# Linear bias attention: the values' projection moved into the first score slots

## The reference

```
qkv = x @ W_attn + b_attn
q, k, v = jnp.split(qkv, 3, axis=-1)             # each to B, T, H, D
att = jnp.einsum('bqhd,bkhd->bhqk', q, k) * scale
att = att / temperature
bias = slopes[:, None, None] * rel[None, :, :]   # rel = key position - query position
bias = jnp.where(causal[None, :, :], bias, -jnp.inf)
att = att + bias[None, :, :, :]
w = jax.nn.softmax(att, axis=-1)
y = jnp.einsum('bhqk,bkhd->bqhd', w, v).reshape(Bc, Tc, Cc)
return y @ W_proj + b_proj
```

## Time and profile before

| | |
|---|---|
| median of 3 runs | 1758.93 us (1758.31 to 1760.62) |
| the profiled execution | 1761.15 us, its span 1759.8 us |
| busy, share of the span | PE 92%, DVE 59%, ACT 51%, POOL 25% |
| mean granted clock of TensorE | 0.982 |
| the stage `l3_attn` in the span | about 1309 to 1454 us |

### The profile page before, as it was taken

The page is one execution under the profiler, slowest core; times in us unless marked ns, Lnnn a source line. Parts: engine busy times, 40 slices in busy tenths (PEclk is TensorE's granted clock), DMA queues, the critical chain, the costliest instruction groups (busy, mean ns, idle before and its releaser), DMA issues. The chain is left out here.

```text
span 1759.8 us, 22408 instructions
## 1 busy us (share of the span) xinstructions
PE 1624.3 (92%) x7539; PEld 830.7 (47%) x7541; DVE 1037.3 (59%) x2130; ACT 902.8 (51%) x1748; POOL 431.3 (25%) x545
## 2 busy tenths in 40 slices
PE   7999998999998789999898999999988989999997
PEld 3344444445664244444345555555533445455546
DVE  5732026483314568888956888888547725565515
ACT  2431214253333457777844778888532654555513
POOL 1000100000000145555411555565301102233300
PEclk9999998999999999999999999999998999999998
DMA  6000100001000000000126231111038202000000
GB/s 231 0 1 0 42 1 1 36 0 48 1 1 19 0 10 18 10 10 10 52 96 216 77 99 28 41 42 28 20 70 242 60 1 91 20 22 12 1 0 25
DMA packets 36664, 74.11 MB, mean 42 GB/s; under 512 B 4427, under 2 KB 23179, under 8 KB 35115
## 3 DMA queue, kind: packets, MB, share of 16 engines
q1 hardware_dynamic: 36550, 72.68, 13.0%
HBM read 55.79 MB, written 16.78 MB: 41 GB/s over the span
## 5 line engine op out<-in xcount | busy, mean ns | idle before, releaser
L2456 POOL TENSOR_TENSOR work<-work,arena_b 128x512 f32<-128x512 f32 x128 | 166.5, 1302 | 129.1 <-ACT work L2313 129.1
L2408 DVE CUSTOM_DVE_ANT_0 ctx_keys<-ps,arena_a 128x1024 f32<-128x1024 f32 x128 | 154.7, 1210 | 0.2 <-PE ps L2189 0.2
L2189 PE MATMUL ps<-identity,ctx_keys 128*128 128x128 f32 x1024 | 142.4, 280 | 10.8 <-ACT work L2313 6.8
L2295 ACT ACTIVATE ctx_keys<-ctx_keys,small 128x1024 f32<-128x1024 f32 x128 | 146.8, 1147 | 0.4 <-DVE small L2408 0.4
L2189 PEld LDWEIGHTS ps<-identity,ctx_keys 128*128 128x128 f32 x1024 | 116.8, 143 | 60.6 <-ACT ctx_keys L2295 20.9
L2420 DVE TENSOR_TENSOR work<-ps,arena_b 128x512 f32<-128x512 f32 x128 | 88.1, 688 | 36.8 <-PE ps L2189 35.4
L3308 POOL TENSOR_SCALAR ctx_keys<-ctx_keys,small 128x128 f32<-128x128 f32 (+3 forms) x128 | 67.0, 536 | 172.5 <-DVE small L3231 172.5
L2313 ACT ACTIVATE work<-ps 128x512 f32<-128x512 f32 x128 | 76.2, 595 | 57.6 <-PE ps L2189 56.0
L1984 POOL TENSOR_SCALAR work<-work 128x1024 f32<-128x1024 int32 x64 | 66.6, 1041 | 112.7 <-DVE work L1937 112.2
L1770 PE MATMUL ps<-work 64*128 64x512 f32 x256 | 72.8, 645 | 16.8 <-DVE work L1937 14.6
L214 ACT ACTIVATE norm_parts<-normed 128x1024 f32<-128x1024 f32 x24 | 25.4, 1056 | 119.7 <-DVE normed L207 119.7
(11 more groups left out here) (405 smaller groups left out, 3400.0 us busy)
## 6 DMA issues: line engine op xcount, KB each, us to landing
work<-parts_k_L_xattn SPq DMA_DIRECT2D x15, 384.0 KB, 4.0
arena_a<-in_mask SPq DMA_DIRECT2D x2, 2048.0 KB, 7.8
arena_b<-in_groupT SPq DMA_DIRECT2D x2, 2048.0 KB, 9.6
head_weights<-in_w_L_xattn SPq DMA_DIRECT2D x8, 449.0 KB, 3.3
arena_a<-in_w_l_attn SPq DMA_DIRECT2D x1, 3072.0 KB, 14.7
head_weights<-in_w_L_attn SPq DMA_DIRECT2D x8, 384.0 KB, 3.1
work<-parts_q_L_attn SPq DMA_DIRECT2D x8, 384.0 KB, 4.6
work<-parts_k_L_attn SPq DMA_DIRECT2D x8, 384.0 KB, 5.4
```

The lines of the kernel that those rows point to most:

```text
L2189: mm = pe.transpose(t_psum[z][:, kt * P:(kt + 1) * P], prob[i % NP][:, o:o + P], k.iden[:, :])
L2295: act.activation(p, p, ACT.Exp, scale=-1.0, bias=minmax[:, i % 8:i % 8 + 1], accum_out=sums[:, i % 8:i % 8 + 1]).then_inc(*exped.up())
L2408: dve.tensor_tensor_reduce(prob[i % NP], s_psum[i % NS], NEG[:, b, qt, :], -1.0, BIG * 3e8, OP.add, OP.min, minmax[:, i % 8:i % 8 + 1]).th ...
L2456: pool.tensor_tensor(p, p, GT[:, b, 4:8, qt * P:(qt + 1) * P], OP.mult).then_inc(*weighed_pool.up())
```

## The change

The values leave the list of jobs; the list itself goes, and the chunks run in order with the six banks in turn. `values_of(pe, t)` stands behind the scores of slots 0 to 7, where the beat was, and makes one tile of 128 tokens: two products as before, and a third of a row of 128 ones with the row of the bias, added in the same accumulation. The tiles go to banks 2 to 5, two in each. In slots 1, 3, 5 and 7 ScalarE copies a bank into `vh` (L2848 has a copy of the same shape); VectorE's adds of the bias are gone. Unit 0's first transposed scores wait for the four copies. VectorE writes the ones at the stage's start. In VectorE's list `ln.scale` for the second half now follows `finish(0)` directly, and `finish(5)` follows the subtraction of chunk 6. SyncE's and GpSimd's orders are untouched.

```diff
-    JOBS = CHUNKS[0:2] + [("v", 0, 0), ("v", 0, 1)] + CHUNKS[2:6] + [("v", 0, 2), ("v", 0, 3)] + CHUNKS[6:8]
+    ones = k.extra[0:1, 1856:1984]
...
 def tensor(pe):
...
-        for y, (what, m, j) in enumerate(JOBS):
-            ps = k.bank(RING[y % 6])
-            if y in (0, 4):
-                pe.wait_ge(*ln.out(1 + y // 4))
-            if y >= 6:
-                pe.wait_ge(*freed(y - 6))
...
-            if y == 1:
+        for x, (what, m, t0) in enumerate(CHUNKS):
+            if x in (0, 2):
+                pe.wait_ge(*ln.out(1 + x // 2))
+            if x >= 6:
+                pe.wait_ge(*plain(x - 6))
+            for c in range(DC):
+                mm = pe.matmul(k.bank(RING[x % 6]), W[what][:, c, m * P:(m + 1) * P], k.Hn[:, c, t0:t0 + S], start=c == 0,
+                               stop=c == 1)
+            mm.then_inc(*part.up())
+            if x == 1:
                 ln.var(pe, 1)
-        pe.wait_ge(*values(nk))
...
-                if s < LAG - 2:
-                    k.beat(o_bank, 1)
+                if s < B * nk:
+                    values_of(pe, s)
...
 def transposed(pe, u, late):
+        if u == 0 and not late:
+            pe.wait_ge(*values(nk))
...
+    def values_of(pe, t):
+
+        if t == 0:
+            pe.wait_ge(*tempered(3))
+        ps = k.bank(2 + t // 2)[:, t % 2 * D:(t % 2 + 1) * D]
+        for c in range(DC):
+            pe.matmul(ps, k.Hn[:, c, t * P:(t + 1) * P], W["v"][:, c, :], start=c == 0, stop=False)
+        pe.matmul(ps, ones, bv[0:1], start=False, stop=True).then_inc(*valued.up())
...
 def scalar(act):
+            if s < B * nk and s % 2:
+                act.wait_ge(*valued(s + 1))
+                if s == 1:
+                    act.wait_ge(*cleared(2))
+                act.activation(vh[:, s - 1:s + 1, :, 0:dh], k.bank(2 + s // 2).rearrange("p (k h d) -> p k h d", k=2, h=H),
+                               ACT.Copy).then_inc(*values.up())
...
 def vector(dve):
+        dve.memset(ones, 1.0).then_inc(*tempered.up())
...
+        for x, (what, m, _) in enumerate(CHUNKS):
+            if what == "q":
+                dve.wait_ge(*part(x + 1))
+                if x >= 3:
+                    dve.wait_ge(*low(x - 2))
+                dve.tensor_scalar(rest[x][0], k.bank(RING[x % 6]), bqk[:, m:m + 1], rt, OP.add, OP.mult).then_inc(*q_plain.up())
+            dve.wait_ge(*hi(x + 1))
+            dve.tensor_tensor(rest[x][1], rest[x][0], parts[x][:, 0, :], OP.subtract).then_inc(*rest1.up())
+            if x not in (0, 2, NC // 2):
+                finish(dve, x - 1)
+            if x == 1:
                 ln.scale(dve, 1)
+            if x in (1, NC // 2 - 1, NC - 1):
+                finish(dve, x)
```

More of the change, by code:

```diff
@@ L2664, in l3_attn @@
     part, valued, scored, turned, scored_t, pv, spread, final = k.signals("pe", 8)
-    k_plain, hi, top_out, top_hi, exped, gathered, logged, inverse = k.signals("act", 8)
-    q_plain, rest1, low, tempered, values, maxed, top_rest, top_low, resid, scaled = k.signals("dve", 10)
+    k_plain, hi, top_out, top_hi, exped, gathered, logged, inverse, values = k.signals("act", 9)
+    q_plain, rest1, low, tempered, maxed, top_rest, top_low, resid, scaled = k.signals("dve", 9)
     middle, cleared, top_mid, put = k.signals("pool", 4)
@@ L2670, in l3_attn @@
     unit = lambda u: (u // 8, u % 8 // 4, u % 4)
-    def freed(y):
-        what, _, j = JOBS[y]
-        return values(j + 1) if what == "v" else plain(CHUNKS.index(JOBS[y]))
     def sync(sp):
@@ L2846, in scalar @@
                     act.wait_ge(*low(x - 2))
-                y = JOBS.index(CHUNKS[x])
-                act.activation(rest[x][0], k.bank(RING[y % 6]), ACT.Identity, bias=bqk[:, 2 + m:3 + m]).then_inc(*k_plain.up())
+                act.activation(rest[x][0], k.bank(RING[x % 6]), ACT.Identity, bias=bqk[:, 2 + m:3 + m]).then_inc(*k_plain.up())
             act.wait_ge(*plain(x))
@@ L2904, in vector @@
         dve.wait_ge(*loaded(7))
[L2905 to L2931, removed]
+        for x, (what, m, _) in enumerate(CHUNKS):
[9 more added lines that the diff above has]
+            if x == 1:
                 ln.scale(dve, 1)
-        finish(dve, pending)
+            if x in (1, NC // 2 - 1, NC - 1):
+                finish(dve, x)
         for s in range(SLOTS):
```

## The result

Over 20 runs each the changed kernel took 1763.59 us (median, 1758.19 to 1766.90) and the kernel before 1759.89 us (1756.65 to 1762.99): ratio 1.0019, 95% interval 1.0012 to 1.0027, so 3.3 us slower (2.1 to 4.8), at the edge of the 0.2% that I had set for "no change". The forecast was 2.0 us slower, in a range of 1757.6 to 1763.6. Put on the median that the forecast started from, the measured ratio gives 1758.93 x 1.0019 = 1762.3 us for the 1760.9 forecast.

What follows compares the result with a forecast made beforehand. Bound: a chain through slots 0 to 4, last_piece, put_top and stores 6 and 7 to unit 0's exponential. Terms -3.3, +2.4, +2.2, +1.15, -0.5 sum to +2.0 us: 1760.9 us from 1758.93, range 1757.6 to 1763.6.

Steps and rivals of the forecast that it cites:

- The chain: Slots 0 to 4, transpose, last_piece, put_top, stores 6 and 7 set unit 0's first exponential (1355.98 us), hence the end.
- Part 1: Projections without the values: ln.scale 1.5 us earlier, VectorE's chain 1.8 us shorter, slot 0 3.3 us earlier.
- Part 2: TensorE's two gaps, before chunk 2 and behind chunk 7: clock falls priced at 1.2 us each, +2.4 us.
- Part 3: Slots lengthen to 2.2 us with the values, +2.2 us over four; slot 4's later transpose, +1.15 us.
- Part 4: Transfers: stores of chunk 1 up to fetch 2 move by +0.3 us, still ahead of the first maxima row.
- Part 5: The clock later, from 1345 us into the steady part: no fall from 1345 to 1360, -0.5 us taken.
- The transfers hold everything: Rival: neither gap costs, last_piece stays nearly as now, fetches and stores wait for each other; 1758.5 us, chance 0.25.
- The values hide wholly: Rival: the products cost the slots nothing, slot 4's first reduction 1.5 us earlier; 1755.7 to 1757.4 us, chance 0.10.
- The clock decides: Rival, TensorE from 1317 to slot 2: both gaps cost 1.7 us, lower clock reaches slots; +5.0, 1763.9 us, chance 0.15.

Runs made afterwards that it cites:

- e2: The changed kernel with 12 beats in the gap between chunks 1 and 2 and 13 more behind chunk 7; ratio 1.0018 to the kernel before.
- e9: The changed kernel with the bias product over 128 rows of 1/128 instead of one row of ones; ratio 1.001 to the kernel before.
- e1: The changed kernel without the product of the ones with the bias row (values lack their bias); ratio 1.001 to the kernel before.
- e3: The changed kernel with the first maxima row (put_top) issued behind the stores of chunk 7, ahead of fetch 3; ratio 1.0015 to the kernel before.
- e5: The changed kernel with fetch 4 issued behind the second maxima row instead of ahead of it; ratio 1.0007 to the kernel before.
- e12: The changed kernel with beats in both gaps, the bias product over 128 rows and fetch 4 behind the second maxima row; ratio 1.0001 to the kernel before.

## Why the prediction was nearly right, step by step

**The chain held up to the exponential of unit 0, not beyond.** last_piece moved by +3.18 us and SyncE's put_top with it (40.78 for 37.60); the exponential waited for the stores as before, and moved by 2.35. It moved less since the last store landed 0.8 us faster after its issue (49.27 - 45.80 for 46.92 - 42.63). But unit 4 moved by 3.02, more than the exponential, so "whatever moves 1355.98 moves the end, and nearly nothing else does" was wrong; part 4 has the other path.

**Part 1** held: -1.5 us forecast for ln.scale, -1.55 measured; -3.3 for slot 0 with the clock up, -2.98 in e2 and e9, so the shorter chain of VectorE gave 1.4 for the 1.8 forecast.

**Part 2**: the clock fell at the first gap in four of the five executions that left it open and untouched (the change, e1, e3, e5, not e9) and cost 1.70 us (26.87 - 25.17), at the second in one of five (e1), and cost 2.0 us (28.90 - 26.87). By these few, 1.4 + 0.4 = 1.8 us for the 2.4 that I took. Six of six earlier gaps had made me price both alike at 1.2: for the second, of 3.06 us, that was three times too much. The Trainium skill (TensorE: Matmul & The Clock Gate, section "Why this matters for your kernels") would have it fall as well; here it fell in one execution of five.

**Part 3 is the step that failed, by its size.** "With 1.36 us the next score starts at 1340.80 ... 2.2 us a slot": measured were 1.59 and 2.43. The upper bound of the bias product, 0.45, was no bound: it took 0.63, and by e1 a slot is 0.72 longer with it. The slots from 0 to 4 gave back 9.73 - 6.64 = 3.09 us for the 2.2 forecast, and behind slot 4 the transpose cost 1.37 for 1.15 (difference 3.12 us after the slot's first reduction for 1.74).

**Part 4 left a path out.** I followed the first maxima row and not the second. SyncE issues fetches 3 and 4 behind stores 6 and 7 and the second row behind them, in both kernels. In the kernel before, the row landed at 53.86, just ahead of its use:

```profile
1354.84 1.17 SPq L2708 DMA_DIRECT2D work<-extra  x2
DMA to landing us min/median/max: 6.7/6.9/6.9
```

In the changed kernel put_top, late by 3.18, moved stores 6 and 7 and fetches 3 and 4 with it: fetch 4's last transfer lands at 56.29 for 53.12, the row right behind it at 57.15 for 53.86, and TensorE waited 1.82 us at unit 4. e5, which takes fetch 4 from ahead of the row, removes this wait alone. That slot 9 issued the row later (49.93 for 45.77) is not what counted: in e9 it is issued 1.5 us sooner than in e2 and lands no sooner. So slots 5 to 8 were late for nothing, as I had written; the second row was late because the first one was, through the transfers that stand between them.

**Part 5** held in sign: no fall in slots 6 to 9, and none in units 1 to 3. The three units from unit 1 to 4 took 6.95 us with the wait of 1.8 in it, for 6.28 before: 1.15 us won for the 0.5 taken. But in the changed kernel the wait for the second row swallows it: the exponential of unit 4 stands 0.74 or 0.75 us behind the row's landing in the change, e2 and e9, and in e1 as well, where the clock did fall in units 1 to 3.

**The sum again**, with measured terms up to unit 4 in the changed kernel's execution: -2.98 (projections) + 1.70 (first gap) + 3.09 (slots) + 1.37 (transpose) - 0.83 (landing) + 1.82 (unit 4) - 1.15 (clock) = 3.02 us, as read directly, and 3.3 (2.1 to 4.8) in the runs. By the second row it is shorter: the row lands 3.29 us later, and 0.27 of this was slack in the kernel before. That the forecast of 2.0 came so near is in part luck: the projections, the slots, the transpose and the missing path made it too small by 0.3, 0.9, 0.2 and 1.8, the gaps, the landing and the clock too large by 0.7, 0.8 and 0.65.

**The rivals.** *The transfers hold everything*: not so, since in e2 the exponential moves with last_piece (1.70 us for 1.70) and in e12 nearly so (2.73 for 3.18); but they hold part, as e9 shows. *The values hide wholly*: refuted by the 0.70 us that VectorE waits in each slot. *The clock decides*: not it, since the slots stayed at the upper clock, and e2, with no fall up to unit 4 in its execution, still measures 1.0018. What stays open is how often each gap falls over many runs, on which the mean rests.

## What to carry to other kernels

Work that leaves a phase bound by other engines gives nothing back there, and the hole it leaves can cost the clock. Before moving it into slots that look half idle, take the wait loop of the slot, here one reduction, one product and the moved work, and not the busy share: 1.59 us went into a place that had room for 0.8. When slots get longer, follow every transfer that they trigger, and what queues behind it, not only the one on today's path. Where two paths end close together, an edit that shortens one of them shows nothing (e9 against e2), and only the edits together take the cost back (e12).

## What the runs showed that I had not expected

A product of one row by 256 columns (two f32 records) took 0.63 us, one over 128 rows 0.43 (e9). The rows of line 2812 fit this: over one row the first weight load begins together with the first product (1333.8 both), over 128 rows 0.2 us ahead of it (1334.4 for 1334.6). The loads take about the same (182 and 190 ns), but ahead of the one-row load the loads pause:

```profile
1333.81 0.29 PEld L2812 LDWEIGHTS ps<-head_weights,extra 1*128 1x128 f32 x2 [0.33 <-issue]
```

Why this load does not start ahead of its product is not shown. The Trainium skill (TensorE: Matmul & The Clock Gate, section "Why this matters for your kernels") has a product over 32 rows take the same time as one over 128; here products over one row took longer, and the measurement decides. The small transfers of the second maxima row landed with the fetch ahead of them: its last one 0.7 to 0.9 us behind fetch 4 in the kernel before, the change, e1, e2 and e9, whenever it had been issued. In the change the three took 5.7 to 6.0 us; with fetch 4 behind them, 2.2 to 3.0 us (e5).
